# Context attention of a two-layer decoder: dividing by the softmax sums behind the weighted values, and a feed-forward issued two steps ahead

## Chip, cores and metric
The kernel runs on one core of one Trainium2 chip. The metric is the device time of one execution in microseconds (us). It is written for the engines directly: TensorE (PE in the profile), VectorE (DVE), ScalarE (ACT), GpSimd (POOL) and SyncE (SP, which issues all DMAs). Each engine executes its own instructions in the order in which the program lists them, and semaphores hold an instruction back until another engine's has finished.

## What is computed
The input `x` is 4 batches of 512 rows of 128 numbers. Six blocks follow one another, each with a layer norm in front and a residual add behind. The change touches the last two.

```python
# fifth block: 16 heads of width 8 over a context of 32 rows per batch
q = query @ Wq + bq;  k, v = split(context @ Wkv + bkv)
scores = einsum('bhid,bhjd->bhij', q, k) * 8 ** -0.5
attn = softmax(where(mask, -inf, scores));  out = einsum('bhij,bhjd->bhid', attn, v)
x = x + merge_heads(out) @ Wout + bout
# sixth block: every linear layer quantizes its input and weight in blocks of 16
scale = maximum(max(abs(xb)) / 6, 1e-12);  xq = nearest_fp4(xb / scale) * scale
h = silu(fp4_linear(ln(x), w_gate)) * fp4_linear(ln(x), w_up)      # 352 wide
x = x + fp4_linear(h, w_down)
```

## The kernel before
The kernel goes through its blocks as stages; the last three overlap at their edges: stage D (the windowed attention of the fourth block), stage E (the context attention) and stage F (the feed-forward). `x` stays in SBUF as `X[:, b]`. PSUM has eight banks of 512 float32 columns, and a planner (`psum_jobs`, `place_jobs`) goes through a list of jobs in the order in which TensorE issues them, gives each the next bank of a named pool, and turns what the bank's last user must have finished into TensorE's waits. There are no costs or due times in it: the order is the order of the lists.

**Stage E** has 16 steps, one for each tile of 128 rows: step n is batch n // 4, tile n % 4. One step is this chain: TensorE multiplies the queries with `KX`, in which each head's keys are laid out so that 16 heads x 32 context rows come out side by side, 512 columns (`eS`, L1755). VectorE scales, adds the mask (L1845) and takes the maximum of each head (L1849). GpSimd subtracts it (L1916). ScalarE takes the exponential (L1819). VectorE sums each head (L1855) and takes the reciprocal (L1856). GpSimd multiplies the tile by it (`normalized`, L1910). TensorE transposes the tile in four pieces (`eT`, L1787), and ScalarE copies them to `PTE` (L1805). When the four tiles of a batch are there, TensorE multiplies them with the values (`eO`, L1763: four accumulated matmuls, each with weights of 128 columns that are zero but for four heads), ScalarE copies the result (`out_copy`, L1810), TensorE projects (`eX`, L1770), VectorE adds to `X` and takes the statistics of the next norm (L2595, L2515, L2518), ScalarE makes the inverse deviation (`rstd`, L2384, L2386), VectorE normalizes (L2525) and quantizes (`quantize_y`, nine instructions from L1949 to L1964), TensorE transposes (`fX`, L1747) and ScalarE copies (L1833).

The loops of the engines are written out by hand, and all work on the same SE tiles, seven in rotation. On VectorE step n is `shift(n)`, `sums(n - 2)`, then what is left of stage D (`d_tail(n)`), then parts of a batch that is two back. TensorE transposes tile n at its step n + 2. `d_tail(7)` waits for the transposed output of stage D's last batch (`out1`, L1458), which TensorE issues after `values(0)`. The values of batch b are taken on TensorE at step 4b + 6.

**Stage F** has 8 steps, each of two tiles. In a step TensorE makes gate and up (`fG`, `fU`, L1975), ScalarE takes SiLU of the gate (L2011), VectorE multiplies the two into the SBUF tile `HF` (L2037) and does the first part of the quantization (L1949 to L1958: reduce, scale, reciprocal, divide, exponent, step, add), GpSimd does the last two instructions of it (L1928, L1934), TensorE transposes `HQ` (`fT`, L2003), ScalarE copies (L2018, L2019), TensorE multiplies with the down weights (`fD`, L1984) and VectorE adds to `X` (L2049, for step n - 2, right behind L2037). TensorE's order in step n is gate and up of n + 1, down of n - 1, transposes of n. Before step 0 three batches have been quantized, and the fourth is quantized in step 2. All jobs of stage F share the eight banks in rotation. SP writes a batch out when its four tiles are final.

The constants, among them the 512-column mask `vhead` with which GpSimd lays out the values `VX` (one instruction per batch), come in one DMA at the start, on which ScalarE's first instruction waits.

## Time and profile before

| | us |
|---|---|
| median of 3 runs | 1257.46 (1251.67 to 1261.60) |
| profiled execution, its own time | 1253.11 |
| span of the profiled execution | 1251.3 |
| mean granted clock of TensorE | 0.955 of full |
| busy in the span: PE / DVE / ACT / POOL | 1121.6 / 903.5 / 878.4 / 627.0 |

The busy shares are means over stages that have different limits; the stages that the change touches are the last 165 us, where the first instruction of stage E on VectorE starts at 1088.46 us and that of stage F at 1174.97 us. In a row of the timeline stand start, duration, engine, line, operation, what it writes and reads, and in brackets how long the engine had been idle and what released it. A matrix product of float32 shows twice as many instructions as the source issues.

### The profile page before, as it was taken

Reading aid. Unit: us, or ns where it says so; the run is one execution under the profiler, and the core shown is the slowest. Engines: PE = TensorE matmul, PEld = TensorE weight load, DVE = VectorE, ACT = ScalarE, POOL = GpSimd, SP = SyncE. Lnnn points to the kernel's source line nnn. Section 1 sums busy time; section 2 is a strip of 40 time slices with the busy share of each in tenths; the row PEclk is TensorE's granted clock in tenths of the full one; section 3 lists DMA queues with packets and bytes.
Section 4 is the critical chain, followed back from the end, with each engine's and each line's share of the span. In section 5 each row is a group of like instructions: output and inputs, shape, how many; then the busy total and the mean of one; then the engine's idle time right before and its main releaser. Section 6 shows DMA issues by size and latency. Waiting matters only on the chain.

```text
span 1251.3 us, 17047 instructions
## 1 busy us (share of the span) xinstructions
PE 1121.6 (90%) x6055; PEld 581.0 (46%) x6055; DVE 903.5 (72%) x1756; ACT 878.4 (70%) x1150; POOL 627.0 (50%) x463
## 2 busy tenths in 40 slices
PE   6999999999999999987888888799988999985765
PEld 3344444444444444432233332277765667653444
DVE  6776677666776677756898988456646777878885
ACT  2999999999979997882666777654655667742411
POOL 2877777777767776693454654014330300154232
PEclk9999999999999998996899999999998999997977
DMA  7200000000000000020000000000001000000000
GB/s 179 70 1 1 1 1 1 1 1 1 1 0 1 1 1 1 1 69 1 18 1 1 1 1 1 1 1 1 1 5 60 1 1 1 1 1 0 1 9 25
DMA packets 25695, 14.48 MB, mean 12 GB/s; under 512 B 14622, under 2 KB 24460, under 8 KB 25484
## 3 DMA queue, kind: packets, MB, share of 16 engines
q1 hardware_dynamic: 25612, 13.39, 3.8%
q8 instruction: 49, 0.80, 0.3%
q14 instruction: 34, 0.28, 0.1%
HBM read 12.34 MB, written 1.05 MB: 11 GB/s over the span
## 4 chain that ended last, share of the span: by engine, by line
PE 33%; POOL 29%; issue 18%; DVE 16%; ACT 2%; POOLq 0%; DMA 0%; SPq 0%; ACTq 0%; DVEq 0%
DVE ARENA L1170 6%; POOL ARENA L2730 6%; POOL ARENA L2728 5%; POOL ARENA L2724 5%; PE PS L1041 5%; POOL ARENA L2754 3%; POOL WQ L2741 3%; PE PS L911 3%; PE PS L1425 2%; PE PS L1015 2%; PE PS L1449 2%; PE PS L843 2%; PE PS L1416 2%; PE PS L859 2%; POOL WQ L2737 2%
## 5 line engine op out<-in xcount | busy, mean ns | idle before, releaser
L2580 DVE TENSOR_SCALAR ARENA<-PS,ARENA 128x512 f32<-128x512 f32 x256 | 171.9, 742 | 51.9 <-PE PS L2217 51.5
L1170 DVE TENSOR_REDUCE ARENA<-PS 128x1 f32<-128x512 f32 x256 | 160.7, 682 | 27.6 <-PE PS L859 26.9
L1086 ACT ACTIVATE ARENA<-PS 128x1024 f32<-128x1024 f32 x128 | 128.7, 1025 | 60.3 <-PE PS L897 60.0
L2398 ACT ACTIVATE ARENA<-ARENA 128x2048 f32<-128x2048 f32 x64 | 121.9, 1911 | 51.6 <-DVE ARENA L2580 51.0
L2217 PE MATMUL PS<-ARENA 64*128 64x512 f32 x512 | 139.7, 644 | 0.0
L2405 ACT ACTIVATE ARENA<-ARENA,consts_sb 128x2048 f32<-128x2048 f32 x64 | 124.7, 1995 | 0.4
L2227 PE MATMUL PS<-ARENA 128*64 128x512 f32 x512 | 119.3, 609 | 1.5 <-issue 1.5
L2411 ACT ACTIVATE ARENA<-ARENA 128x2048 f32<-128x2048 f32 x64 | 118.4, 1899 | 0.0
L1351 POOL TENSOR_TENSOR ARENA<-ARENA 128x512 f32<-128x512 f32 x32 | 40.7, 1270 | 119.8 <-DVE ARENA L1309 119.3
L2737 POOL TENSOR_SCALAR WQ<-ARENA,consts_sb 128x512 bf16<-128x512 f32 x32 | 22.2, 692 | 146.5 <-DVE ARENA L2556 146.5
L859 PE MATMUL PS<-ARENA 32*128 32x512 bf16 x256 | 71.9, 404 | 26.1 <-DVE ARENA L1170 20.7
L2556 DVE TENSOR_SCALAR ARENA<-PS 128x512 f32<-128x512 f32 x32 | 22.1, 691 | 97.5 <-PE PS L2192 97.5
L911 PE MATMUL PS<-ARENA 128*32 128x512 f32 x512 | 71.7, 632 | 9.3 <-issue 8.4
L2730 POOL TENSOR_TENSOR ARENA<-ARENA 128x1024 f32<-128x1024 f32 x32 | 76.0, 2374 | 2.5
L2728 POOL TENSOR_TENSOR ARENA<-ARENA 128x1024 f32<-128x1024 f32 x32 | 75.8, 2368 | 0.0
L2724 POOL TENSOR_TENSOR ARENA<-ARENA 128x1024 f32<-128x1024 f32 x32 | 75.6, 2362 | 0.0
L2227 PEld LDWEIGHTS PS<-ARENA 128*64 128x64 f32 x512 | 34.8, 139 | 81.8 <-issue 81.8
L1323 POOL TENSOR_SCALAR ARENA<-ARENA,consts_sb 128x512 bf16<-128x512 f32 x32 | 21.7, 692 | 96.4 <-ACT ARENA L1068 96.4
L1041 PEld LDWEIGHTS PS<-W,ARENA 128*128 128x128 f32 x512 | 59.5, 192 | 21.2 <-issue 18.9
L1117 ACT ACTIVATE ARENA<-PS,ARENA 128x512 f32<-128x512 f32 x64 | 40.4, 684 | 37.5 <-PE PS L1015 37.4
L1041 PE MATMUL PS<-W,ARENA 128*128 128x128 f32 x512 | 65.3, 281 | 0.8 <-ACT ARENA L1117 0.7
L859 PEld LDWEIGHTS PS<-ARENA 32*128 32x128 bf16 x256 | 17.6, 92 | 103.7 <-DVE ARENA L1170 63.6
(301 smaller groups left out, 2589.7 us busy)
## 6 DMA issues: line engine op xcount, KB each, us to landing
ARENA<-in_window_bias_dram SPq DMA_DIRECT2D x1, 1536.0 KB, 6.4
WKVG<-in_L_attn_W_in_dram SPq DMA_DIRECT2D x3, 384.0 KB, 5.4
X<-in_x_dram SPq DMA_DIRECT2D x4, 256.0 KB, 3.9
W<-in_L_ffn_w_dram SPq DMA_DIRECT2D x1, 1024.0 KB
out_dram<-X SPq DMA_DIRECT2D x4, 256.0 KB, 2.3
BV<-in_L_attn_b_in_dram SPq DMA_DIRECT2D x1, 512.0 KB, 6.1
Wout<-in_L_attn_W_out_dram SPq DMA_DIRECT2D x1, 512.0 KB, 4.8
WQ<-in_L_attn_wq_dram SPq DMA_DIRECT2D x1, 512.0 KB, 3.5
```

What stands on the lines that cost most here:

```text
L1041: mm = pe.matmul(o[:, t * P:(t + 1) * P], H1[:, i % 2, c, t * P:(t + 1) * P], W2[:, e, c, :], start=c == 0, stop=c == 1)
L1086: act.activation(PT[m % PT_SLOTS], bank(("cP", m)), ACT.Exp, scale=0.5).then_inc(sem("c_exp"), 1)
L1170: dve.tensor_reduce(NMX[:, w % 2, t, h:h + 1], bank(("cS", n, j)), AX.X, ALU.max, negate=True).then_inc(sem("c_max"), 1)
L2217: done(pe.matmul(banks[c], SK[r, u % 2, kt * P:(kt + 1) * P], MQ[r, u % 2, :], start=False, stop=True), ("S", u, c))
L2227: mm = pe.matmul(o[hd * 64:hd * 64 + 64, :], VA[:, u % 3, kt, hd * 64:hd * 64 + 64], D[:, u % 2, kt, hd, :], start=kt == 0, stop=kt == QT - 1)
L2398: act.activation(chunk(u, half), chunk(u, half), ACT.Sqrt).then_inc(sem("rooted"), 1)
L2405: act.activation(chunk(u, half), chunk(u, half), ACT.Ln, bias=const("eps_w")).then_inc(sem("logged"), 1)
L2411: act.activation(chunk(u, half), chunk(u, half), ACT.Exp, scale=-2.0).then_inc(sem("w_ready"), 1)
L2580: dve.tensor_scalar(D[:, u % 2, kt, hd, :], bank(("S", u, c)), K2[:, u % 2, kt, hd:hd + 1], 1e-30, ALU.add, ALU.max).then_inc(sem("guarded ...
L2724: pool.tensor_tensor(WSUM[:, u % 2], D[:, u % 2, 0], D[:, u % 2, 1], ALU.add).then_inc(sem("w_paired"), 1)
L2728: pool.tensor_tensor(WPAIR, D[:, u % 2, 2], D[:, u % 2, 3], ALU.add).then_inc(sem("w_paired"), 1)
L2730: pool.tensor_tensor(WSUM[:, u % 2], WSUM[:, u % 2], WPAIR, ALU.add).then_inc(sem("w_summed"), 1)
```

## The change
In stage E the exponentials are no longer divided by their sums before the transposes. TensorE transposes them as they are, one step earlier (tile n at step n + 1, waiting for `e_exp`), and the SE tiles are six. The values are now laid out as 32-column blocks, one for each group of four heads, so that `eO` is four matmuls of 32 output rows each, and a second product of the same form with the new, 32-column `vhead` gives the sums of the heads, repeated over each head's eight rows (`eZ`). ScalarE inverts them (`invert_sums`: Ln, then Exp of minus that), and VectorE multiplies `eO` by it (`weighted`), in place of ScalarE's copy. `sums` on VectorE and `normalized` on GpSimd are gone. The stages of a batch are issued later: the projection one batch later than the values, the add two steps further, `normalize` and `quantize_y` behind that, so that only batches 0 and 1 are quantized before stage F and batches 2 and 3 within its steps 1 and 2.

In stage F gate and up are issued two steps ahead, and TensorE's order in step n is down of n - 1, gate and up of n + 2, transposes of n. Each kind of job has banks of its own (`fT` two, `fG` two, `fU` four), and the product with the down weights goes to the free columns of the `fT` banks. The product of SiLU and up is written back to the banks of `fU`, with the block maxima beside it, and read from there. The add for step n - 2 sits behind the division. In the last step VectorE does what GpSimd did, in two halves, and transposes, copies, products and adds follow by halves.

The diff, cut to its core:

```diff
-    for g in range(4):
-        vmask[:, g, :] = (part[None, :] // DX == (4 * g + head)[:, None])
-    cols["vhead"] = vmask.reshape(P, -1)
+    cols["vhead"] = (part[:, None] // CK == np.arange(4 * DX)[None, :] // DX).astype(np.float32)
...
+    def values(b, pool):
+        return [(("eO", b), 1, [("e_o", b + 1)], pool), (("eZ", b), 1, [("e_sum", b + 1)], pool)]
+
+    def project_out(b, pool):
+        return [(("eX", b), 1, [("x_new", 4 * B + b + 1)], pool)]
+
     jobs = scores(0, "E3") + scores(1, "E3")
...
+    for s in range(steps + 1):
         jobs += d_tail(s)
         for n in scores_at(s):
             jobs += scores(n, pool_at(s))
...
+        if s >= 1:
+            b, t = divmod(s - 1, QT)
+            jobs += [(("eT", s - 1), 1, [("e_pt", s)], pool_at(s))]
             if t == 1 and b:
...
+                jobs += values(b - 1, pool_at(s))
+            if t == 1 and b >= 2:
+                jobs += project_out(b - 2, pool_at(s))
+            if s == FIRST_QUANTIZED:
+                jobs += [(("fX", 0), 1, [("f_x", 1)], pool_at(s))]
+    jobs += values(B - 1, "E2") + gate_and_up_jobs(0) + project_out(B - 2, "E01") + project_out(B - 1, "E01")
+    return jobs + [(("fX", 1), 1, [("f_x", 2)], "fG")]
+
+
+FIRST_QUANTIZED = 15
 
 
 def gate_and_up_jobs(n):
...
+    return [(("fG", n), 2, [("f_silu", n + 1)], "fG"), (("fU", n), 2, [("f_scaled", n + 1)], "fU")]
...
+    jobs = gate_and_up_jobs(1)
+    last = B * QT // 2 - 1
+    for n in range(last + 1):
+        if n in QUANTIZED_AT:
+            jobs += [(("fX", QUANTIZED_AT[n]), 1, [("f_x", QUANTIZED_AT[n] + 1)], "fG")]
+        if n + 2 <= last:
+            jobs += gate_and_up_jobs(n + 2)
+        if n < last:
+            jobs += [(("fT", n), 2, [("f_ht", n + 1), ("x_final", n + 1)], "fT")]
+        else:
+            jobs += [(("fL", j), 1, [("f_ht", last + 1 + j)], "fG") for j in range(2)]
+    return jobs
+
+
+QUANTIZED_AT = {2: B - 2, 4: B - 1}
...
             def values(b):
                 pe.wait_ge(sem("e_pt"), QT * (b + 1))
-                pe.wait_ge(sem("e_vx"), b + 1)
+                pe.wait_ge(sem("e_vx"), 1)
                 o = begin(("eO", b))
                 for g in range(4):
-                    mm = pe.matmul(o, VX[b][:, g, :], PTE[:, b % 2, g, :], start=g == 0, stop=g == 3)
+                    r = slice(32 * g, 32 * g + 32)
+                    mm = pe.matmul(o[r, :], VX[:, b, r], PTE[:, b % 2, g, :], start=True, stop=True)
                 done(mm, ("eO", b))
+                o = begin(("eZ", b))
+                for g in range(4):
+                    r = slice(32 * g, 32 * g + 32)
+                    mm = pe.matmul(o[r, :], const("vhead"), PTE[:, b % 2, g, :], start=True, stop=True)
+                done(mm, ("eZ", b))
...
+            for s in range(STEPS + 1):
                 d_tail(s)
                 for n in scores_at(s):
                     scores(n)
...
+                if s < 1:
                     continue
...
+                n = s - 1
                 b, t = divmod(n, QT)
...
+                pe.wait_ge(sem("e_exp"), n + 1)
                 o = begin(("eT", n))
...
+                p = SE[n % 6].rearrange("p h j -> p (h j)")
                 for g in range(4):
                     mm = pe.transpose(o[:, g * P:(g + 1) * P], p[:, g * P:(g + 1) * P], ident)
                 done(mm, ("eT", n))
...
+                if t == 1 and b:
                     values(b - 1)
...
+                if t == 1 and b >= 2:
+                    project_out(b - 2)
+                if s == FIRST_QUANTIZED:
+                    turn_quantized(pe, begin, done, 0)
+            values(B - 1)
             pe.wait_ge(sem("f_w"), 3)
             gate_and_up(pe, begin, done, 0)
...
+            project_out(B - 2)
             project_out(B - 1)
...
+            turn_quantized(pe, begin, done, 1)
...
+            def invert_sums(b):
+                full(act, ("eZ", b))
+                if b:
+                    act.wait_ge(sem("e_o"), b)
+                act.activation(ISUM, bank(("eZ", b)), ACT.Ln).then_inc(sem("e_sum"), 1)
+                act.wait_ge(sem("e_sum"), b + 1)
+                act.activation(ISUM, ISUM, ACT.Exp, scale=-1.0).then_inc(sem("e_isum"), 1)
+
+            for n in range(STEPS + 2):
                 b, t = divmod(n, QT)
                 d_tail(n)
...
                 if n < STEPS:
                     act.wait_ge(sem("e_shift"), n + 1)
...
+                    act.activation(SE[n % 6], SE[n % 6], ACT.Exp).then_inc(sem("e_exp"), 1)
+                if n >= 2:
+                    turned(n - 2)
+                if t == 3 and b:
+                    invert_sums(b - 1)
+                if t == 2 and b >= 2:
+                    rstd(5, b - 2)
+                if n == FIRST_QUANTIZED + 1:
+                    quantized_out(act, 0)
+            invert_sums(B - 1)
+            silu(act, 0)
...
-            def sums(n):
-                dve.wait_ge(sem("e_exp"), n + 1)
-                if n >= 3:
-                    dve.wait_ge(sem("e_p"), n - 2)
-                link(dve.tensor_reduce(SUE[:, n % 3], SE[n % 7], AX.X, ALU.add))
-                dve.reciprocal(RCE[:, n % 3], SUE[:, n % 3]).then_inc(sem("e_rc"), 1)
...
+            def weighted(b):
+                full(dve, ("eO", b))
+                dve.wait_ge(sem("e_isum"), b + 1)
+                if b >= 2:
+                    full(dve, ("eX", b - 2))
+                dve.tensor_tensor(OTE[:, b % 2], ISUM, bank(("eO", b)), ALU.mult).then_inc(sem("e_o"), 1)
+
+            def add(b):
+                dve.wait_ge(sem("xb4"), b + 1)
+                add_to_stream(4, b, ("eX", b))
+                stats(5, b)
+
+            for n in range(STEPS):
                 b, t = divmod(n, QT)
...
+                shift(n)
                 d_tail(n)
...
+                if t == 1 and b >= 2:
+                    weighted(b - 2)
+                if t == 3 and b >= 2:
+                    add(b - 2)
+                if t == 0 and b == 3:
+                    normalize(5, 0)
+                if t == 1 and b == 3:
+                    quantize_y(dve, link, 0)
+            normalize(5, 1)
+            weighted(B - 2)
+            quantize_y(dve, link, 1)
+            weighted(B - 1)
             hidden(dve, link, 0, None)
...
+            add(B - 2)
+            add(B - 1)
...
+            pool.tensor_tensor(VX.rearrange("p b (g c) -> p (b g) c", g=4),
+                               V4.rearrange("p b (g c) -> p (b g) c", g=4),
+                               const("vhead").unsqueeze(1).to_broadcast([P, 4 * B, 4 * DX]), ALU.mult).then_inc(sem("e_vx"), 1)
...
-            def normalized(n):
-                pool.wait_ge(sem("e_rc"), n + 1)
-                pool.tensor_tensor(SE[n % 7], SE[n % 7], RCE[:, n % 3].unsqueeze(2).to_broadcast([P, HX, CK]),
-                                   ALU.mult).then_inc(sem("e_p"), 1)
...
-            for n in range(STEPSF):
+            for n in range(STEPSF - 1):
...
+            def down(n, halves=(0, 1)):
+                for j in halves:
+                    pe.wait_ge(sem("f_ht"), n + 1 + (j if n == last else 0))
                     for c, (r0, k) in enumerate(FCH):
...
+                        mm = pe.matmul(sum_of(n, j), HQT[0:k, n % 2, j, c * P:(c + 1) * P], WD[0:k, c, :],
                                        start=c == 0, stop=c == 2)
...
+                    if n == last or j == 1:
+                        mm.then_inc(sem("f_d"), 1)
+
+            def turn_half(o, n, j):
+                for c, (r0, k) in enumerate(FCH):
+                    mm = pe.transpose(o[0:k, c * P:(c + 1) * P], HQ[:, n % 2, j, r0:r0 + k], ident)
+                return mm
+
+            gate_and_up(pe, begin, done, 1)
             for n in range(STEPSF):
...
+                if n in QUANTIZED_AT:
+                    turn_quantized(pe, begin, done, QUANTIZED_AT[n])
                 if n:
                     down(n - 1)
...
+                if n + 2 < STEPSF:
+                    gate_and_up(pe, begin, done, n + 2)
+                if n < last:
+                    pe.wait_ge(sem("f_hq"), n + 1)
+                    o = begin(("fT", n))
+                    for j in range(2):
+                        mm = turn_half(o[:, j, :], n, j)
+                    done(mm, ("fT", n))
+                else:
+                    for j in range(2):
+                        pe.wait_ge(sem("f_hq"), n + 1 + j)
+                        done(turn_half(begin(("fL", j)), n, j), ("fL", j))
+            for j in range(2):
+                down(last, (j,))
...
+            quantized_out(act, 1)
+            silu(act, 1)
+            act.preload_act_table_set("natural_log_exp_and_others")
+            rstd(5, B - 2)
+            rstd(5, B - 1)
+            turned(0)
+            silu(act, 2)
+            for n in range(1, last):
+                if n in QUANTIZED_AT:
+                    quantized_out(act, QUANTIZED_AT[n])
+                if n + 2 < STEPSF:
+                    silu(act, n + 2)
                 turned(n)
+            act.wait_ge(sem("f_d"), last - 1)
+            for j in range(2):
+                full(act, ("fL", j))
+                act.copy(HQT[:, last % 2, j, 0:2 * P], bank(("fL", j))[:, 0:2 * P])
+                act.copy(HQT[0:96, last % 2, j, 2 * P:3 * P], bank(("fL", j))[0:96, 2 * P:3 * P]).then_inc(sem("f_ht"), 1)
...
+            rows = bank(("fU", n))
+            h = rows[:, :, 0:FI]
+            dve.tensor_tensor(h, SG[:, n % 2], h, ALU.mult).then_inc(sem("f_h"), 1)
+            dve.wait_ge(sem("f_h"), n + 1)
+            scratch = X_SCRATCH[n % 2]
+            blocks = FI // BLK
+            v = h.rearrange("p t (k i) -> p t k i", i=BLK)
+            amax = rows[:, :, FI:FI + blocks]
+            sc, rc = (scratch[0][:, k, 0:2 * blocks].rearrange("p (t k) -> p t k", t=2) for k in (1, 2))
+            A, M, T = scratch[1:4]
+            link(dve.tensor_reduce(amax, v, AX.X, ALU.max, apply_absolute_value=True))
             if n >= 2:
...
+                dve.wait_ge(sem("f_hq"), n - 1)
+            link(dve.tensor_scalar(sc, amax, float(np.float32(1 / 6)), 1e-12, ALU.mult, ALU.max))
+            link(dve.reciprocal(rc, sc))
+            dve.scalar_tensor_tensor(out=A.rearrange("p (t k i) -> p t k i", t=2, i=BLK), in0=v, scalar=1.0 - 2.0 ** -24,
+                                     in1=rc.unsqueeze(3).to_broadcast([P, 2, blocks, BLK]),
+                                     op0=ALU.mult, op1=ALU.mult).then_inc(sem("f_scaled"), 1)
+            if n >= 1:
+                add()
+            dve.wait_ge(sem("f_scaled"), n + 1)
+            link(dve.tensor_scalar(M.bitcast(U32), A.bitcast(U32), 0x7F800000, None, ALU.bitwise_and))
+            link(dve.tensor_scalar(M, M, 1.0, 3.0 * 2.0 ** 21, ALU.max, ALU.mult))
+            dve.tensor_tensor(T, A, M, ALU.add).then_inc(sem("f_added"), 1)
...
+            def between(n):
+                if n >= 2:
+                    add(n - 2)
+                if n in (1, 2):
+                    normalize(5, B - 3 + n)
+                    quantize_y(dve, link, B - 3 + n, n)
+
+            for n in range(1, STEPSF):
+                hidden(dve, link, n, lambda: between(n))
+            scratch = X_SCRATCH[last % 2]
+            by = lambda t, j: t[:, j * FI:(j + 1) * FI].rearrange("p (k i) -> p k i", i=BLK)
+            blocks = FI // BLK
+            dve.wait_ge(sem("f_added"), last + 1)
+            link(dve.tensor_tensor(scratch[3], scratch[3], scratch[2], ALU.subtract))
+            full(dve, ("fT", last - 2))
+            hq = HQ[:, last % 2].rearrange("p t n -> p (t n)")
+            for j in range(2):
+                scales = scratch[0][:, 1, j * blocks:(j + 1) * blocks].unsqueeze(2).to_broadcast([P, blocks, BLK])
+                if j:
+                    dve.wait_ge(sem("f_hq"), last + 1)
+                else:
+                    dve.wait_ge(sem("f_hq"), last)
+                dve.tensor_tensor(by(hq, j), by(scratch[3], j), scales, ALU.mult).then_inc(sem("f_hq"), 1)
+            add(last - 1)
+            b, t = divmod(2 * last, QT)
+            for j in range(2):
+                dve.wait_ge(sem("f_d"), last + 1 + j)
+                dve.tensor_tensor(X[:, b, t + j], X[:, b, t + j], sum_of(last, j), ALU.add).then_inc(sem("x_final"), 1)
```

## Rows read from the trace of the kernel before
**Rows 1.** Windows: stretch, length, busy us (instructions) PE, PEld, DVE, ACT, POOL, clock, DMA.
```profile
1083.80:1127.00 43.20, 36.23 (x154) 20.68 (x152) 34.12 (x76) 21.10 (x62) 18.90 (x18) 0.99 0.00 1
1127.00:1169.00 42.00, 25.18 (x86) 14.03 (x86) 34.76 (x80) 13.41 (x27) 17.05 (x17) 0.77 0.00 0
1169.00:1239.80 70.80, 50.88 (x218) 36.02 (x218) 62.92 (x105) 18.00 (x31) 22.02 (x16) 0.83 0.04 12
1239.80:1251.30 11.50, 4.47 (x18) 3.74 (x18) 0.42 (x1) 0.85 (x2) 2.76 (x2) 0.59 0.07 23
```
**Rows 2.** Timeline of VectorE in stage E: the sums of a tile, and two waits.
```profile
1102.95 0.68 DVE L1855 TENSOR_REDUCE ARENA<-ARENA 128x16 f32<-128x512 f32 x1
...
1103.84 0.63 DVE L1845 SCALAR_TENSOR_TENSOR ARENA<-PS,BXV 128x512 f32<-128x512 f32 x1
...
1119.30 0.69 DVE L2595 TENSOR_TENSOR X<-X,PS 128x512 f32<-128x512 f32 x1 [6.39 <-PE PS L1458]
...
1143.95 0.69 DVE L1845 SCALAR_TENSOR_TENSOR ARENA<-PS,BXV 128x512 f32<-128x512 f32 x1 [3.64 <-PE PS L1755]
```
**Rows 3.** Groups by line, shapes apart, from 960 us to the end.
```profile
L1910 POOL TENSOR_TENSOR ARENA<-ARENA 128x512 f32<-128x512 f32 x16 | 17.8, 1113 | 3.9 <-DVE ARENA L1856 3.9
...
L1958 DVE TENSOR_TENSOR ARENA<-ARENA 128x704 f32<-128x704 f32 x8 | 7.1, 893 | 0.3
...
L2037 DVE TENSOR_TENSOR ARENA<-ARENA,PS 128x704 f32<-128x704 f32 x8 | 7.1, 882 | 4.7 <-PE PS L1975 4.4
```
**Rows 4.** Costliest groups of the page, whole span: other stages' instructions of similar form.
```profile
L2580 DVE TENSOR_SCALAR ARENA<-PS,ARENA 128x512 f32<-128x512 f32 x256 | 171.9, 742 | 51.9 <-PE PS L2217 51.5
...
L911 PE MATMUL PS<-ARENA 128*32 128x512 f32 x512 | 71.7, 632 | 9.3 <-issue 8.4
```
**Rows 5.** Timeline of TensorE: values of batches 0 and 1.
```profile
1115.13 3.70 PE L1763 MATMUL PS<-ARENA,WQ 128*128 128x512 f32 x8 [0.39 <-ACT ARENA L1805]
...
1134.82 5.89 PE L1763 MATMUL PS<-ARENA,WQ 128*128 128x512 f32 x8
```
**Rows 6.** Timeline of VectorE in stage F.
```profile
1187.63 3.66 DVE L2525 TENSOR_SCALAR Y<-X,MV,RSTD 128x128 f32<-128x128 f32 x4
...
1203.65 0.88 DVE L2037 TENSOR_TENSOR ARENA<-ARENA,PS 128x704 f32<-128x704 f32 x1
...
1209.45 0.89 DVE L2037 TENSOR_TENSOR ARENA<-ARENA,PS 128x704 f32<-128x704 f32 x1
...
1211.50 1.08 DVE L1952 TENSOR_SCALAR ARENA<-ARENA 128x44 f32<-128x44 f32 x1
...
1218.97 0.89 DVE L2037 TENSOR_TENSOR ARENA<-ARENA,PS 128x704 f32<-128x704 f32 x1 [2.96 <-PE PS L1975]
```
**Rows 7.** Timeline of GpSimd in stage F.
```profile
1209.40 1.68 POOL L1928 TENSOR_TENSOR ARENA<-ARENA 128x704 f32<-128x704 f32 x1 [9.31 <-DVE ARENA L1958]
1211.15 1.38 POOL L1934 TENSOR_TENSOR ARENA<-ARENA 128x704 f32<-128x704 f32 x1
```
**Rows 8.** Timeline of TensorE in stage F.
```profile
1212.59 1.54 PE L2003 MATMUL PS<-consts_sb,ARENA 128*128 128x128 f32 x6 [3.71 <-POOL ARENA L1934]
...
1220.05 0.82 PE L2003 MATMUL PS<-consts_sb,ARENA 128*128 128x128 f32 x6
1220.70 2.53 PE L1975 MATMUL PS<-WKVG,ARENA 128*128 128x352 f32 x8
1223.07 1.50 PE L1984 MATMUL PS<-Wout,ARENA 128*128 128x128 f32 x12
...
1245.17 2.93 PE L1984 MATMUL PS<-Wout,ARENA 128*128 128x128 f32 x12 [0.94 <-ACT ARENA L2019]
```
**Rows 9.** Timeline of VectorE: the last two instructions.
```profile
1239.35 0.41 DVE L2049 TENSOR_TENSOR X<-X,PS 128x256 f32<-128x256 f32 x1
1248.14 0.42 DVE L2049 TENSOR_TENSOR X<-X,PS 128x256 f32<-128x256 f32 x1 [8.38 <-PE PS L1984]
```
**Rows 10.** Chain that ended last, start of the program: start, us, what.
```profile
1.24 4.44 DMA consts_sb<-in_consts_dram
```

183 lines of the change are left out of this document (30 added, 153 removed).

## Prediction
> **What bounds the kernel now.** I read the windows first, for the stages that the change touches. From 1127 us on TensorE is busy 25.18 of 42.00 us and then 50.88 of 70.80, at a granted clock of 0.77 and 0.83, and GpSimd and ScalarE less than half of the time. VectorE is busy 34.76 and 62.92 [rows 1]: it sets the pace, and about 4 of the 15.1 us that it lacks are gaps between linked instructions. Then VectorE's timeline, for its waits: 6.39 us for stage D's last output, 3.64 for scores [rows 2], 2.96 for gate and up [rows 6]. Between its two adds at the very end there are 8.38 us with nothing to do, the chain of the last step through GpSimd, TensorE and ScalarE [rows 9]. So there are four terms: the start, what delays 1119.30, the 120.05 us from there to 1239.35, and the 11.95 us from there to the end of the span.
>
> **Start.** The constants are 448 columns narrower of some 930. Their DMA takes 4.44 us and ends on the chain that ended last [rows 10]. Half the bytes can't save half of it, since the statistics of the first batch come in beside them: 0.5 us, between 0 and 1.
>
> **Before 1119.30.** VectorE waits for the transposes of stage D's output, and TensorE has `values(0)` in front of them: 3.70 us [rows 5]. The new form is eight source matmuls, 16 recorded ones, of 32 output columns. The nearest row is stage C's, 512 of this very form in 71.7 us busy, 0.14 each although one lasts 632 ns, so four column groups run side by side [rows 4]. That is 8 x 0.14 = 1.1 us for `eO`, 1.1 for `eZ`, and 1.5 less. The transposes no longer wait for a sum (0.89 from one instruction to the next [rows 2]) and a multiplication on GpSimd (1.1 [rows 3]), but tile 5 is transposed in front as well (half a us). I take -2.0; 0 if stage D's own work decides, -4 if all adds up.
>
> **From there to the last hidden step (120.05 us).** Removed from VectorE: ten sums (tiles 6 to 15; the others lie in front) x 0.89 = 8.9. Added: four `weighted`, each a 512-column product with a PSUM source like L2595, 0.69 [rows 2]: 2.8. Net -6.1. GpSimd's multiplications, ScalarE's copies and `VX` are off the path and cost or save nothing there: POOL is busy 17.05 of 42 us [rows 1]. ScalarE gets two activations per batch (0.6 to 0.7 each) for one copy; three of the four are covered by its own slack, the fourth is counted below.
>
> Port conflicts: the 44-column instruction at 1211.50 took 1.08 us and ended 0.05 behind GpSimd's L1934 at 1212.53, so it was held until GpSimd had finished [rows 6, 7]. Four short normalizing instructions took 3.66 us in the same way [rows 6]. Counted over stages E and F this makes some 10.9 us: 1 to 1.3 for each of three norms behind L1910, two times 0.5 in `quantize_y`, and 6.5 in stage F. After the change L1910 is gone, the scales of a hidden step are computed from PSUM, and the division reads PSUM; I keep 2.5, for norms behind the shift that stays on GpSimd. -8.4, with ends of 0 (the PSUM forms are held too, and other norms fall beside GpSimd) and -10.9.
>
> Waits of VectorE now: 11.2. New ones, with t = 0 at the new 1119.30. VectorE does add, two shifts, `normalize(4,3)` (held 1 us), `weighted(0)`, shifts 10 and 11 and stands at `add(0)` at 9.8. TensorE can begin the transposes of that norm at 6.5, then tile 9, `values(1)` and only then `project_out(0)`: at the half clock, in which `values(1)` now runs (5.89 against 3.70 [rows 5]), 1.1 + 1.1 + 3.6 + 1.4, so 14. **4.2 us of wait.** The inverse deviation of that batch sits in ScalarE's order ahead of its copy of the last queries, so the scores for shift 12 come another 2.5 later. Then `normalize(5,1)` and `weighted(2)`, one behind the other behind the loop, wait for ScalarE 0.6 and 1.6; the last sums and the table load in front of `silu(0)` leave some 2; 1 more for TensorE in stage F. In all 12: +0.8. Ends: 6 (full clock, short queue) and 20 (each wait lasts as long as 3.64 did, or 2.96, in six places).
>
> The quantizations of batches 2 and 3 only move; each is nine instructions in either place. But they now sit in the middle of hidden steps 1 and 2, behind which `f_added` is late for GpSimd, and gate and up are by then two steps ahead: nothing waits.
>
> Writing the product to PSUM is shown by no row. The reading product with PSUM source takes 882 ns against 893 from SBUF [rows 3], so 0 for reads. Upper bound: the scalar operation of rows 4, 742 ns for 512 columns, scaled to 704: 1.02 us, 0.14 over 0.88, three accesses in eight steps: 3.4. I take 0, the row of the same form. The Trainium skill says otherwise ("VectorE: DVE Perf Modes", on the errata): a VectorE instruction has a fixed cost of 58 cycles from SBUF and 120 from PSUM, which speaks against keeping the product there. By that rule three accesses would cost an estimated 0.2 us a step, 1.6 us in all. The 882 and 893 ns of rows 3 don't bear it out.
>
> In steps 3 to 7 of stage F, VectorE's own length is 5.80 (1203.65 to 1209.45 [rows 6]). TensorE's is a new loop, because `down` now stands directly behind ScalarE's copy of the transposes: 0.82 + about 1.15 for the copies + 1.50 + 2.53 [rows 8] = 6.0. The lead of two steps covers the difference five times over, 1 us. This term: -6.1 - 8.4 + 0.8 = -13.7.
>
> **End.** Now 11.95 us from 1239.35 [rows 9], of which 2.75 lie behind the last add. In between are GpSimd's 3.1 [rows 7], transposes 1.5, copies 0.95, products 2.93 at half clock [rows 8] and semaphores. New: subtraction 0.89, one half 0.5, the second 0.5, transposes 0.45, copies 0.6, products 0.75 to 1.5, add 0.3, semaphores 0.5, so about 4.8. 11.95 - 2.75 - 4.8 = 4.4, taken as -4.3 (ends -2.5 and -5.5).
>
> **Sum**: -0.5 - 2.0 - 13.7 - 4.3 = -20.5. Against the profiled execution's 1253.11 this is 1232.6, against the median of 1257.46 it is 1237. The runs spread over 10 us, so I take 1236.
>
> **Rivals.**
> - *The waits come back.* Same mechanism, but the serial places take 20 us instead of 12 and the port conflicts return half: +8 + 3, 1247, about 1% under the median. For it: ScalarE's order has `rstd` and the copies between exponentials, TensorE's clock is already 0.77 there. Against: most of VectorE's 16 shifts need nothing of them. Chance 0.18.
> - *Larger gain*: waits of 6 instead of 12, 4 us in front: 1228. For it: TensorE has 5 us less work in `values`. Chance 0.13.
> - *Slower: TensorE's loop in stage F.* Place: `down`, gate and up, transposes in one serial round with ScalarE's copy inside. If the clock stays at the half level, a round is 1.54 + 1.15 + 2.93 + 5.06 = 10.7 instead of 6.0 [rows 8]; over seven rounds +33, so 1269. It decides from a round of about 9.0, where the 20.5 are used up ((9.0 - 6.0) x 7 = 21). Against it: the round leaves TensorE idle for 1.1 us at a time, while the half-clock rows stand behind idle times of 3.71 us [rows 8]. Chance 0.05.
> - *The products don't run side by side.* If the 16 records cost 0.46 each as in rows 5, `values` takes 7.4 instead of 2.2, on the path at three places: +15.6, 1252. Rows 4 speak against it. Chance 0.04.
>
> **Numbers.** The forecast has 0.60. Its own range is 1230 to 1242; with the rivals at both sides and the spread of the runs the range is 1223 to 1250. A change of less than 1% (12.6 us, so down to 1244.9) can't be told from none. Faster by over 1%: forecast, larger gain and a third of the first rival, 0.80. Within: 0.15. Slower by over 1%: 0.05.
>
> **What would show it.** The 6.39 us wait in front of stage D's last add shrinks to 2 to 4 us plus what VectorE arrives earlier. `eO` and `eZ` show 16 records in 2 to 4 us. A wait of 3 to 5 us on L1770's successor in front of `add(0)`. Hidden steps 3 to 7 start 5.8 to 6.2 us apart with no 1.08 us instruction, and the clock of TensorE in stage F is over 0.9. From the last addition of step 7 to the end 7 to 9 us instead of 11.95. I am wrong if VectorE still waits for over 18 us in all, or if a step of stage F takes over 7.

## Result and the profile after the change

The kernel after takes 1237.82 us (median of 4 runs, 1234.46 to 1239.04), the kernel before 1258.31 us beside it (4 runs): ratio 0.9845 [0.9804, 0.9886]. A second comparison gave 1234.67 against 1255.44 us, ratio 0.9851 [0.9811, 0.9890]. The forecast was 1236 us within 1223 to 1250, and 20.5 us of gain; the differences of the medians are 20.5 and 20.8 us. The execution profiled after took 1239.04 us with a span of 1237.2.

The two spans differ by only 14.1 us. The stages that the change does not touch explain the rest. VectorE's first shift of scores, where stage E begins for it, stands at 1088.46 us before and at 1092.87 after, 4.4 us later; from there to the end it is 162.84 us before and 144.33 after, 18.5 us less. In the twelve further profiles the same first shift lies anywhere from 1084.56 to 1097.94 us, while the length behind it repeats to a few tenths where neither code nor clock differs: 144.33, 143.96 and 144.04 us in three profiles of the same work. Of the kernel before there is one profile only, so how far its own 162.84 us would repeat isn't known. Every number below therefore counts from that shift or from stage D's last add to the stream, and not from the start of the span.

The windows of the kernel after, cut at the same times as [rows 1] as far as the shorter span allows (stretch, length, busy us and instructions of PE, PEld, DVE, ACT, POOL, clock, DMA share, GB/s):

```profile
1083.80:1127.00 43.20, 38.01 (x186) 22.25 (x184) 29.14 (x58) 24.12 (x68) 10.89 (x11) 1.00 0.00 1
1127.00:1169.00 42.00, 29.17 (x142) 15.10 (x142) 30.45 (x67) 17.75 (x34) 8.39 (x8) 0.80 0.00 1
1169.00:1230.00 61.00, 38.10 (x186) 28.52 (x187) 57.65 (x113) 16.01 (x30) 21.41 (x14) 0.85 0.05 14
1230.00:1237.20 7.20, 4.15 (x24) 3.52 (x22) 1.73 (x5) 1.06 (x4) 0.00 (x0) 0.74 0.12 36
```

GpSimd's busy time in stage E is halved (17.05 to 8.39 us in the second line). In stage F VectorE is busy 57.65 of 61.00 us, 95%, where it was 62.92 of 70.80: it is still what sets the pace, with less idle time. TensorE's clock is hardly higher than before, 0.80 and 0.85.

TensorE in front of stage D's last add, timeline. The values of batch 0 are the first line and the sums the second:

```profile
1119.52 1.06 PE L1769 MATMUL PS<-ARENA,WQ 128*32 128x512 f32 x8
1120.40 1.04 PE L1774 MATMUL PS<-ARENA,consts_sb 128*32 128x512 f32 x8
1121.37 0.66 PE L1464 MATMUL PS<-consts_sb,ARENA 128*128 128x128 f32 x4
```

The 16 records take 1.9 us together, where eight took 3.70 [rows 5]: eight records that write 32 partitions each, of about 0.6 us, fit into 1.06 us, so the column groups run side by side. They still stand in front of the transposes (third line) that the add needs.

VectorE from that add to the first hidden step, timeline; a number in brackets is the wait before the instruction, with what ended it:

```profile
1122.06 0.69 DVE L2663 TENSOR_TENSOR X<-X,PS 128x512 f32<-128x512 f32 x1 [4.92 <-PE PS L1464]
...
1126.60 1.84 DVE L2593 TENSOR_SCALAR Y<-X,MV,RSTD 128x128 f32<-128x128 f32 x4
...
1135.36 0.69 DVE L2663 TENSOR_TENSOR X<-X,PS 128x512 f32<-128x512 f32 x1 [3.69 <-PE PS L1781]
...
1139.73 0.69 DVE L1859 SCALAR_TENSOR_TENSOR ARENA<-PS,BXV 128x512 f32<-128x512 f32 x1 [2.36 <-PE PS L1760]
...
1153.21 0.69 DVE L2663 TENSOR_TENSOR X<-X,PS 128x512 f32<-128x512 f32 x1 [0.74 <-PE PS L1781]
...
1155.82 1.12 DVE L2593 TENSOR_SCALAR Y<-X,MV,RSTD 128x128 f32<-128x128 f32 x4 [0.60 <-ACT RSTD L2454]
1158.03 0.69 DVE L1870 TENSOR_TENSOR ARENA<-ARENA,PS 128x512 f32<-128x512 f32 x1 [1.09 <-issue]
...
1164.49 0.69 DVE L1870 TENSOR_TENSOR ARENA<-ARENA,PS 128x512 f32<-128x512 f32 x1 [0.75 <-ACT ARENA L1826]
...
1166.51 0.90 DVE L2069 TENSOR_TENSOR PS<-ARENA,PS 128x704 f32<-128x704 f32 x1 [1.32 <-ACT ARENA L2030]
```

The wait for stage D's output is 4.92 us instead of 6.39 [rows 2]. Behind it stand the waits that the forecast placed: 3.69 in front of the first new add, 2.36 in front of shift 12, and small ones behind the loop.

Stage F, timelines of VectorE and, in the second block, of GpSimd:

```profile
1205.25 0.90 DVE L2069 TENSOR_TENSOR PS<-ARENA,PS 128x704 f32<-128x704 f32 x1
1206.18 0.90 DVE L2077 TENSOR_REDUCE PS<-PS 128x44 f32<-128x704 f32 x1
1207.12 0.20 DVE L2080 TENSOR_SCALAR ARENA<-PS 128x44 f32<-128x44 f32 x1
1207.35 0.43 DVE L2081 RECIPROCAL ARENA<-ARENA 128x44 f32<-128x44 f32 x1
...
1211.33 0.90 DVE L2069 TENSOR_TENSOR PS<-ARENA,PS 128x704 f32<-128x704 f32 x1 [0.22 <-PE PS L1982]
```
```profile
1205.20 1.68 POOL L1939 TENSOR_TENSOR ARENA<-ARENA 128x704 f32<-128x704 f32 x1 [2.71 <-DVE ARENA L2090]
1206.95 1.39 POOL L1945 TENSOR_TENSOR ARENA<-ARENA 128x704 f32<-128x704 f32 x1
```

The 44-column instruction runs inside GpSimd's second product and takes 0.20 us; in the kernel before it took 1.08 in the one step of [rows 6] and 1.07 in another. The reciprocal behind it reads SBUF, also inside that product, and isn't lengthened: 0.43 us, as without GpSimd beside it. The five hidden steps that begin with step 3 start 5.84, 6.08, 5.85 and 5.84 us apart.

The end, VectorE's and TensorE's timelines:

```profile
1229.68 1.08 DVE L2123 TENSOR_TENSOR ARENA<-ARENA 128x352 f32<-128x352 f32 x2
...
1233.56 0.29 DVE L2128 TENSOR_TENSOR X<-X,PS 128x128 f32<-128x128 f32 x1 [1.99 <-PE PS L1995]
```
```profile
1230.90 1.49 PE L2002 MATMUL PS<-consts_sb,ARENA 128*128 128x128 f32 x6
```

The wait of 8.38 us between the last two adds [rows 9] has become a subtraction and the multiplication in two halves on VectorE itself (first line: the halves) and a wait of 1.99. The last transposes take 1.49 us, about what they took at the half clock in [rows 8]; the clock here is 0.69 in the 5.5 us behind hidden step 7.

One table carries the comparison. "Front" is from the first shift to stage D's last add, "middle" from there to the end of hidden step 7, "busy" VectorE's busy time in the middle, "waits" the sum of its bracketed waits there, "end" the rest of the span. The rows below the second are the experiments of the next section.

| kernel | front | middle | busy | waits | end | all |
|---|---|---|---|---|---|---|
| before | 30.84 | 120.13 | 104.80 | 11.20 | 11.87 | 162.84 |
| after | 29.19 | 106.66 | 91.68 | 10.77 | 8.48 | 144.33 |
| after, again | 29.19 | 106.29 | 91.61 | 10.48 | 8.48 | 143.96 |
| wider constants | 29.20 | 106.29 | 91.59 | 10.50 | 8.55 | 144.04 |
| eight sums back | 29.20 | 109.85 | 96.78 | 8.60 | 8.52 | 147.57 |
| multiplication on GpSimd back | 29.19 | 109.20 | 94.47 | 10.58 | 9.56 | 147.95 |
| product in SBUF | 29.19 | 111.97 | 97.80 | 9.89 | 9.60 | 150.76 |
| lead of one step | 29.18 | 131.01 | 91.59 | 35.68 | 10.57 | 170.76 |
| last step through GpSimd | 29.19 | 108.23 | 91.70 | 12.33 | 11.85 | 149.27 |
| down last | 29.20 | 105.01 | 91.61 | 9.14 | 8.76 | 142.97 |
| rstd a step later | 29.19 | 102.89 | 91.63 | 7.07 | 8.51 | 140.59 |
| the same, second profile | 29.20 | 102.52 | 91.54 | 6.85 | 7.45 | 139.17 |
| values and rstd a step later | 27.19 | 106.82 | 90.69 | 11.98 | 7.41 | 141.42 |
| the same, rstd ahead | 27.19 | 103.64 | 91.60 | 7.85 | 7.48 | 138.31 |

The end varies with TensorE's clock alone where its code is the same: 7.4 to 7.5 us in three profiles at 1.00 behind step 7, 8.5 at 0.69, 9.6 at 0.55 and 0.60, and 10.6 at 0.50 (lead of one step). So that part of a difference in the last two columns is clock and not the edit.

### The profile page after: what moved, and what is told of

The parts are those of the page before. It is cut to its first block, busy times and chain, and to the rows that moved or that the text cites. A ratio compares the mean times of both kernels' runs of the same rounds, so it can differ in the third digit from the quotient of the medians.

```text
span 1237.2 us, 17060 instructions
## 1 busy us (share of the span) xinstructions
PE 1116.8 (90%) x6087; PEld 575.5 (47%) x6087; DVE 888.1 (72%) x1732; ACT 881.2 (71%) x1156; POOL 604.0 (49%) x442
## 4 chain that ended last, share of the span: by engine, by line
PE 35%; POOL 27%; DVE 18%; issue 16%; ACT 3%; DMA 0%; POOLq 0%; DVEq 0%; ACTq 0%
DVE ARENA L1176 6%; POOL ARENA L2798 6%; POOL ARENA L2796 5%; POOL ARENA L2792 5%; PE PS L1047 5%; POOL ARENA L2822 3%; POOL WQ L2809 3%; PE PS L917 3%; PE PS L1431 2%; PE PS L849 2%; PE PS L1021 2%; PE PS L1455 2%; PE PS L1422 2%; PE PS L865 2%; POOL WQ L2805 2%
```

## Experiments

Each kernel is the kernel after with one edit, unless the text says otherwise.

**The narrower constants.** 480 unused columns bring the width back.

```
     cols["xhead"] = ...
+    cols["unused"] = np.zeros((P, 480))
```

> The changed kernel with 480 unused columns of constants added, so that the first DMA is as large as it was before. If the smaller DMA at the start is worth 0.5 us, ScalarE's first instruction starts 0.5 us later than in the changed kernel (5.2 us), and the first scores of the first block as well. The rival says that the start is set by the first batch's own DMA and statistics: no difference. In neither case does anything behind the first block move by more than executions differ.

Median 1231.1 us (2 runs), ratio 0.9791 [0.9752, 0.9830]: no loss. The constants landed in 4.4 us before, 3.1 after and 3.7 here, although before and here they are the same 465 KB, and ScalarE's first activation, at 5.71 before, shows why that is free (its timeline, the kernel after and this one):

```profile
5.20 0.30 ACT L2452 ACTIVATE RSTD<-MV,consts_sb 128x4 f32<-128x4 f32 x1 [3.19 <-DVE MV L2586]
```
```profile
5.10 0.30 ACT L2453 ACTIVATE RSTD<-MV,consts_sb 128x4 f32<-128x4 f32 x1 [3.09 <-DVE MV L2587]
```

In both it waits for the statistics (MV) and not for the constants. The half microsecond between the kernels is there in the traces, but the width doesn't bring it back; why the transfer took 4.4 us in the one profile before stays open.

**The sums.** Reduction and reciprocal on VectorE, with results that nobody reads, for tiles 6 to 13 behind stage D's add (and tiles 0 to 5 in front).

```
+                if n >= 2:
+                    sums(n - 2)
                 d_tail(n)
```

> The changed kernel with the two removed VectorE instructions per tile put back (sum of each head and its reciprocal, tiles 0 to 13, results unused). If VectorE's own work is what the stage is made of, the eight tiles behind stage D's last add cost 8 x 0.89 = 7.1 us less what falls into its waits: the sums of steps 10 and 11 disappear in the 3.69 us wait in front of the first context add, so about +5 us between that add of stage D (1122.06) and the end of hidden step 7 (1228.72), 106.7 us now. If the waits for TensorE and ScalarE set the pace, under +2 us.

Median 1242.02 us, ratio 0.9881 [0.9850, 0.9911]. The middle is 3.2 us longer, between the 5 of the theory and the under 2 of its rival. VectorE's timeline:

```profile
1123.45 0.68 DVE L1881 TENSOR_REDUCE ARENA<-ARENA 128x16 f32<-128x512 f32 x1
1124.16 0.25 DVE L1882 RECIPROCAL ARENA<-ARENA 128x16 f32<-128x16 f32 x1
1124.33 0.63 DVE L1861 SCALAR_TENSOR_TENSOR ARENA<-PS,BXV 128x512 f32<-128x512 f32 x1
...
1126.48 1.18 DVE L2602 TENSOR_SCALAR Y<-X,MV,RSTD 128x128 f32<-128x128 f32 x4
...
1134.56 0.69 DVE L2672 TENSOR_TENSOR X<-X,PS 128x512 f32<-128x512 f32 x1 [1.96 <-PE PS L1783]
```

One sum takes 0.88 us of VectorE (1123.45 to 1124.33), eight take 7.0. Two things give about half of it back: the waits fall by 2.2 us, above all that of 3.69 to 1.96, and the two norms that fell beside GpSimd's subtraction no longer do (1.18 against 1.84 for the one shown, 1.3 us for both). So the removed work was worth less than its duration, mostly because a wait follows it.

**The multiplication on GpSimd.** It writes to an unused tile, behind each exponential; VectorE waits for it before it overwrites that exponential's tile six steps later.

```
+                if n >= 2:
+                    pool.wait_ge(sem("e_exp"), n - 1)
+                    pool.wait_ge(sem("e_p"), n - 2)
+                    pool.tensor_tensor(DUM, SE[(n - 2) % 6], ..., ALU.mult).then_inc(sem("e_p"), 1)
```

> The changed kernel with GpSimd's multiplication of each tile put back at its old place (behind the subtraction of the tile two later), writing to an unused tile. VectorE only has to wait for it before it overwrites a tile six steps later. If port conflicts of VectorE with GpSimd were a part of the gain, the normalizing and scaling instructions beside it get longer by up to 1 us each: +2 to +4 us between stage D's last add and the end of hidden step 7. If GpSimd is simply off the path: 0. If its queue matters (its subtraction comes 1 us later): scores tiles reach ScalarE later and the 3.69 us wait grows by 1.

Median 1238.70 us, ratio 0.9858 [0.9828, 0.9888]. Middle +2.5, VectorE's busy time +2.8 with the same 191 instructions, waits about the same. (The end is 1.1 longer, which is the clock.) VectorE's timeline has the place:

```profile
1126.88 3.25 DVE L2600 TENSOR_SCALAR Y<-X,MV,RSTD 128x128 f32<-128x128 f32 x4
```

The four normalizing instructions take 3.25 us instead of 1.84: GpSimd now works without a gap from 1126.73 to 1129.79, in three instructions, and three of the four end within 0.1 us of the end of one of them. The add behind comes 1.3 us later. So the price is VectorE held; GpSimd's queue being late would have lengthened the first wait, which is 3.56 us against 3.69.

**The product in SBUF.** Product, maxima and division use SBUF again.

```
-            dve.tensor_tensor(h, SG[:, n % 2], h, ALU.mult)
+            dve.tensor_tensor(HF, SG[:, n % 2], h, ALU.mult)
```

> The changed kernel with the product of SiLU and up written to an SBUF tile, as before, and the block maxima too; the semaphores are as in the changed kernel. If reading from PSUM keeps VectorE free of GpSimd, the 44-column scaling instruction, which starts 1.9 us into a step, waits again until GpSimd's second instruction ends 3.2 us into it: about +1.3 us in each of the steps 2 to 7 that have GpSimd's work beside them, a step of 7.1 us instead of 5.83, +6 to +8 us in all. If the PSUM form is only as fast as the SBUF form and nothing else, 0. If a PSUM access costs more, as the fixed costs in the Trainium skill (VectorE: DVE Perf Modes) would have it, this version is faster by 0.2 us a step.

Median 1244.94 us, ratio 0.9903 [0.9870, 0.9935]: of all edits that keep the order of the work this costs most. VectorE's timeline of stage F, and GpSimd's in the last block:

```profile
1204.70 0.89 DVE L2070 TENSOR_TENSOR ARENA<-ARENA,PS 128x704 f32<-128x704 f32 x1
1205.62 0.89 DVE L2078 TENSOR_REDUCE ARENA<-ARENA 128x44 f32<-128x704 f32 x1
1206.55 1.28 DVE L2081 TENSOR_SCALAR ARENA<-ARENA 128x44 f32<-128x44 f32 x1
...
1208.32 0.89 DVE L2083 SCALAR_TENSOR_TENSOR ARENA<-ARENA 128x704 f32<-128x704 f32 x1
```
```profile
1206.40 1.38 POOL L1946 TENSOR_TENSOR ARENA<-ARENA 128x704 f32<-128x704 f32 x1
```

Only the 44-column instruction changes: 1.28 us instead of 0.20, and it ends 0.05 us behind GpSimd's product. Steps 3 to 7 start 6.90 or 6.91 us apart instead of 5.84. In the middle VectorE is busy 6.1 us longer, six times 1.07 us less a little, and waits 0.9 less: that is its +5.3. The theory had taken 1.3 us a step and 6 to 8 in all; it had the place right and the size too large. The three wide accesses cost 0.89 here and 0.90, 0.90 and 0.89 in PSUM, so the third theory, that PSUM costs 0.2 us a step, finds 0.02.

**The lead of two steps.** Gate and up products one step ahead, as before, and ScalarE's SiLU with them.

```
-                if n + 2 < STEPSF:
-                    gate_and_up(pe, begin, done, n + 2)
+                if n + 1 < STEPSF:
+                    gate_and_up(pe, begin, done, n + 1)
```

> The changed kernel with gate and up issued one step ahead instead of two (TensorE: down of n - 1, gate and up of n + 1, transposes of n). If the lead of two steps is what keeps VectorE from waiting in stage F, gate and up of step n + 1 now come only behind GpSimd's end of step n - 1, the transposes, ScalarE's copies (1.15 us) and the down products (1.5): 3.7 + 0.8 + 1.15 + 1.5 + 1.3 for the gate + 0.8 for SiLU is 9.2 us into a step of 5.83, so VectorE waits some 3.4 us in each of steps 3 to 7, +15 to +20 us. If the banks of their own for each kind of job are what matters, under +3 us.

Median 1265.58 us, ratio 1.0066 [1.0041, 1.0090]: slower than the kernel before. VectorE's busy time is unchanged (91.59 us), its waits rise from 10.8 to 35.7, more than the 15 to 20 us expected. Its timeline, and TensorE's behind it:

```profile
1230.32 0.90 DVE L2068 TENSOR_TENSOR PS<-ARENA,PS 128x704 f32<-128x704 f32 x1 [6.74 <-PE PS L1982]
```
```profile
1221.80 1.52 PE L2002 MATMUL PS<-consts_sb,ARENA 128*128 128x128 f32 x6 [4.02 <-DVE X L2098]
```

In the kernel after and here the down product lies in the banks of the transposes, so the transposes of a step wait for VectorE's add of the step before (4.02 us; the expectation had left this out), and gate and up of the next step stand behind them. A round is then 10.9 to 12.7 us. In the kernel after the same wait is there (1.36 us in front of the transposes of step 6), but there gate and up of the next step have gone ahead. I read from this that the second step of lead pays for the shared banks; no run has one step of lead with separate banks, so how much of the 24.9 us the sharing makes isn't shown.

**The last step.** Through GpSimd and in one piece again.

```
-            for n in range(STEPSF - 1):
+            for n in range(STEPSF):
...
+            add(last - 1)
+            add(last)
```

> The changed kernel with its last step done as all others: GpSimd does the last two quantizing instructions, and transposes, copies, down products and add come in one piece. If the forecast's reckoning of the end holds, GpSimd's 3.1 us takes the place of VectorE's 1.4 to the first half, and the pipelining by halves is gone: about +3.5 us from the end of hidden step 7 to the end of the span (8.5 us now), so 12. The rival, that the halves bring nothing because each small instruction has its fixed cost, says +1.7.

Median 1238.32 us (2 runs), ratio 0.9859 [0.9819, 0.9899]; the medians don't resolve it, the profile does. The end is 11.85 us instead of 8.48, +3.4 at nearly the same clock (0.71 and 0.69), with the old wait back (VectorE's timeline):

```profile
1236.97 0.42 DVE L2085 TENSOR_TENSOR X<-X,PS 128x256 f32<-128x256 f32 x1 [6.64 <-PE PS L1992]
```

The middle, which this edit doesn't touch, is 1.6 us longer because one step takes 7.73 us; on that step see the experiment on TensorE's loop.

**Inverse deviation a step later.** In the kernel after ScalarE's `rstd(5, 0)` waits 4.79 us for the statistics with the copy of the last queries behind it (ScalarE's timeline of the kernel after):

```profile
1137.41 0.30 ACT L2452 ACTIVATE RSTD<-MV,consts_sb 128x4 f32<-128x4 f32 x1 [4.79 <-DVE MV L2586]
...
1137.85 0.67 ACT L1537 ACTIVATE ARENA<-PS,BN 128x512 f32<-128x512 f32 x1
```

```
-                if t == 2 and b >= 2:
+                if t == 3 and b >= 2:
                     rstd(5, b - 2)
```

> The changed kernel with ScalarE's inverse deviation of a batch (two short activations that wait for the context add) one step later in its order, behind the copy of the last queries. If the waits of VectorE at the first context add and at shift 12 come from this serial order, the copy of the queries is no longer held from 1136.1 to 1137.9, shift 12 starts 1.1 us earlier (wait 2.36 becomes 1.2), and the values of the last batch 1 us earlier: -1 to -2.5 us. If TensorE is the cause, 0.

> The kernel after with ScalarE's rstd(5, b) one step later, repeated in the same call as the kernel with the later values, to compare the two improved versions on one chip. Expected: 140.6 us from the first scores shift to the end again (every variant has repeated to tenths of a microsecond there), median ratio to before 0.976 to 0.983; if the version with later values and rstd ahead of invert_sums works, this one is 3 to 5 us slower than it.

Median 1230.29 us (2 runs), ratio 0.9795 [0.9763, 0.9827], and in a second comparison 1231.67 us (6 runs), ratio 0.9833 [0.9806, 0.9859]. All behind stage D's add is 3.7 and 5.2 us shorter than in the kernel after, where 1 to 2.5 was expected. VectorE's timeline of the first:

```profile
1131.29 0.69 DVE L1859 SCALAR_TENSOR_TENSOR ARENA<-PS,BXV 128x512 f32<-128x512 f32 x1 [0.69 <-PE PS L1760]
...
1148.15 1.11 DVE L2593 TENSOR_SCALAR Y<-X,MV,RSTD 128x128 f32<-128x128 f32 x4 [1.97 <-ACT RSTD L2454]
```

The wait for shift 12 falls from 2.36 to 0.69. The gain beyond the expectation lies behind it: five waits of 4.50 us in all in the kernel after have become one of 1.97, for the second `rstd`, moved too, in front of the norm of batch 1, and one of 0.38.

The two profiles of this one kernel also differ, by 1.6 us between stage D's add and the first new one (13.29 and 11.67 us). TensorE's timeline of the values, first the first profile, then the second:

```profile
1124.21 1.94 PE L1769 MATMUL PS<-ARENA,WQ 128*32 128x512 f32 x8
1125.92 1.48 PE L1774 MATMUL PS<-ARENA,consts_sb 128*32 128x512 f32 x8
```
```profile
1125.88 1.06 PE L1769 MATMUL PS<-ARENA,WQ 128*32 128x512 f32 x8
1126.76 1.04 PE L1774 MATMUL PS<-ARENA,consts_sb 128*32 128x512 f32 x8
```

The second holds the upper level of 2.4 GHz, in the first the clock has fallen toward 1.2 GHz in this stretch, in front of which TensorE had waited 2.90 us in both. The windows from 5 to 10 us behind stage D's add, in the same order:

```profile
1120.30:1125.30 5.00, 2.89 (x20) 1.90 (x24) 4.53 (x8) 2.81 (x7) 2.14 (x3) 0.81 0.01 2
```
```profile
1122.33:1127.33 5.00, 2.88 (x28) 1.71 (x28) 4.54 (x8) 2.81 (x7) 2.14 (x3) 1.00 0.01 2
```

VectorE, ScalarE and GpSimd do the same work; TensorE's busy time is the same too, but at the granted clock of 0.81 it gets through 20 records where at 1.00 it gets through 28. The second profile's end is 1.1 us shorter for the same reason, and one of its steps in stage F is 0.8 longer (7.04 against 6.20): 3.7 us is what the edit itself shows.

**Values a step later as well**, so that stage D's transposes go first. The projection now stands in front of the values, and the first `invert_sums` runs at ScalarE's step 8.

```
-                if t == 1 and b:
-                    values(b - 1)
...
+                if t == 2 and b:
+                    values(b - 1)
```

> The changed kernel with ScalarE's inverse deviation one step later, and on TensorE the projection of the batch before in front of the values, and the values one step later than now (with their inversion at ScalarE's step 8 for batch 0). If the serial places found in the changed kernel cost what they show, stage D's transposed output comes 2.1 us earlier (eO and eZ no longer in front of it), the 3.69 us wait for the first context add nearly goes, and shift 12 comes about 4 us earlier: -4 to -7 us against the changed kernel. The rival: VectorE's waits only move to the next place (the values and their inverted sums come later, so weighted() waits), and it is within 2 us.

Median 1232.88 us, ratio 0.9829 [0.9802, 0.9856]. Stage D's add comes 2.0 us earlier and its wait is 2.91 instead of 4.92, but the whole is 141.42 us: 2.9 less than the kernel after, not the 4 to 7 expected, and more than with `rstd` alone. VectorE's timeline, then ScalarE's:

```profile
1133.99 1.12 DVE L2594 TENSOR_SCALAR Y<-X,MV,RSTD 128x128 f32<-128x128 f32 x4 [3.49 <-ACT RSTD L2455]
...
1151.68 1.11 DVE L2594 TENSOR_SCALAR Y<-X,MV,RSTD 128x128 f32<-128x128 f32 x4 [5.09 <-ACT RSTD L2455]
```
```profile
1132.27 0.60 ACT L1824 ACTIVATE ARENA<-PS 128x512 f32<-128x512 f32 x1 [3.40 <-PE PS L1774]
```

The inverse deviation (at 1133.43) stands behind `invert_sums` (the row shown), which waits for the later sums. So the next kernel turns the two round on ScalarE:

```
                 if t == 3 and b >= 2:
+                    rstd(5, b - 2)
                     invert_sums(b - 1)
-                    rstd(5, b - 2)
```

> Change of the kernel after: the values and sums products of batches 0 to 2 are issued one step later, invert_sums(0) runs at step 8, and ScalarE takes rstd(5, b) at step t = 3, now AHEAD of invert_sums(b + 1) instead of behind it. Theory (what held the previous attempt back was the order of these two on ScalarE: the values products that invert_sums waits for are a step later, and the normalizing of VectorE queued behind them for 3.49 and 5.09 us): both waits fall to about 1 us, so from the first scores shift to the end 135 to 137.5 us instead of 141.4 there and 140.6 with rstd(5, b) moved alone; stage D's last add stays at about +27.2. Rival (the waits are set by the statistics themselves or by TensorE's products, not by the queue of ScalarE): 140 to 142 us, as before.

Median 1232.09 us (4 runs), ratio 0.9821 [0.9803, 0.9838]; 138.31 us from the first shift on, inside neither theory (135 to 137.5; 140 to 142). The cause of the two waits was the queue: the wait of 3.49 us is gone and that of 5.09 is down to 0.82, but 2.73 us have moved on to the product of the weighted values (VectorE's timeline):

```profile
1148.94 1.11 DVE L2594 TENSOR_SCALAR Y<-X,MV,RSTD 128x128 f32<-128x128 f32 x4 [0.82 <-ACT RSTD L2455]
...
1152.78 0.69 DVE L1871 TENSOR_TENSOR ARENA<-ARENA,PS 128x512 f32<-128x512 f32 x1 [2.73 <-issue]
```

Its stretch is 6.0 us shorter than that of the kernel after, 1.0 of it by the clock in the end. It is 2.3 us shorter than the first profile with `rstd` alone and 0.9 shorter than the second, which has the same full clock at the values and in the end; 3 to 5 were expected. All four medians of these variants (1230.29 to 1232.88) lie below both of the kernel after (1234.67 and 1237.82), but so does that of the padded kernel (1231.1), which does the same work as the kernel after, and the intervals of the ratios overlap. That they are faster is shown in the stretch, not in the time of the whole.

**The order of TensorE's loop.** Gate and up of step n + 2 stand before the down product of step n - 1.

```
-                if n:
-                    down(n - 1)
                 if n + 2 < STEPSF:
                     gate_and_up(pe, begin, done, n + 2)
+                if n:
+                    down(n - 1)
```

> The kernel after with TensorE's loop of the feed-forward reordered: the gate and up products of step n + 2 stand before the down product of step n - 1, not behind it. My theory (VectorE sets the hidden steps at 5.84 us each, TensorE has room in every step): hidden steps 3 to 7 stay at 5.8 to 5.9 us, and the time within 1 us of after. Rival (TensorE's loop is as near to being the bound as VectorE's, at a half clock in part of the stage): some steps grow or shrink by 0.5 us or more, 2 us or more in all.

Median 1237.62 us, ratio 0.9868 [0.9839, 0.9897]. From the first new add to the end of step 7 it is 93.34 us, in the kernel after 93.36. Its steps 3 to 7 start 5.84, 5.84, 6.87 and 5.85 us apart. These four add up to 24.4 us, against 23.6 in the kernel after and 23.8 in its repetition, so stage F is 0.6 to 0.8 us longer here. The equal sum comes from the wait of 0.74 us in front of the second add, which this profile lacks, as does the kernel after in its repetition.

One step longer than 5.85 is in every profile with a lead of two steps but that of the product in SBUF, and it has two causes. In the kernel after (6.08) and in others (6.24, 7.04, 7.73) VectorE waits there for gate and up, and TensorE is at the lower clock: 0.54 in the 7 us around the step of 7.04. Here the clock is 1.00 throughout the step of 6.87. VectorE waits for the down product, which now stands behind gate and up, and these had waited for ScalarE's copy of the quantized rows (VectorE's timeline, then TensorE's):

```profile
1210.01 0.42 DVE L2099 TENSOR_TENSOR X<-X,PS 128x256 f32<-128x256 f32 x1 [0.94 <-PE PS L1995]
```
```profile
1206.03 2.60 PE L1982 MATMUL PS<-WKVG,ARENA 128*128 128x352 f32 x8 [1.04 <-ACT ARENA L1847]
```

So VectorE sets the steps of 5.84, and TensorE is the next limit, when its clock is low or when the product that VectorE needs first stands second. The rival was right that a step grows by over 0.5 us, and wrong that 2 us come together.

**The kernel after, again.**

> The kernel after itself, unchanged, timed again in five rounds. Theory (the change is worth what its own stages show, 18 to 20 us, and what differs besides is scatter of the unchanged stages): median 1232 to 1239 us, ratio 0.981 to 0.988; from the first scores shift to the end 144.3 us, or 1.6 us less, since two other runs in which this stretch is the same code had the last add of stage D to the first add of the new stage once at 13.30 and once at 11.67 us. Rival (the first comparison was lucky): ratio above 0.990.

Ratio 0.9851 [0.9811, 0.9890], 143.96 us from the first shift on, 13.30 us between stage D's last add and the first new one: the theory holds.

## Why the prediction was right

**Start, -0.5.** The constants are 480 columns narrower (465 and 225 KB), not 448. The traces differ by the half microsecond, but the padded kernel starts as early, so the width isn't its reason. The term isn't confirmed and too small to matter.

**Before stage D's last add, -2.0: measured -1.65.** The step was right: `eO` and `eZ` take 1.9 us for 3.70. Its other half, that TensorE must then do more in front, holds too: with the values moved behind the transposes a further 2.0 us come free, so TensorE's order in front of this add is still what decides.

**Middle, -13.7: measured -13.5**, though its three parts were each a little off and cancel; that the sum fits to 0.2 us is luck. Work and port conflicts together were -14.5; VectorE's busy time fell by 13.1. Waits were +0.8; they fell by 0.4.
- *Port conflicts*, VectorE's instructions held beside GpSimd's, were the larger part, and the mechanism is borne out: 1.07 us a step by the product in SBUF, 2.8 us by the multiplication on GpSimd. My count of 10.9 us before was too high: against the same forms undisturbed the rows of that trace have some 9.4 us behind stage D's add, because the three norms of stage E lost 0.7 to 0.8 each and not 1 to 1.3. Of the 2.5 us that I left, 1.5 were there (two norms of 1.84 instead of 1.11). That is -7.9 for -8.4. The experiments don't split this gain: in the kernel before, the 44-column instruction was held in two steps of eight (1.08 and 1.07 us), while in the new order, where GpSimd's products lie beside VectorE's in six steps, the SBUF form is held in all six.
- *Removed sums* were taken at their full 0.89 each. The duration was right (0.88), the value was not: 7.0 us put back cost 3.2. The balance came out because I had also counted the waits that the shorter work uncovers, by their places: 4.2 forecast in front of the first add (3.69), 2.5 for shift 12 (2.36), 0.6 and 1.6 behind the loop (0.60, 1.09), 2 in front of the first step (0.75 and 1.32), 1 in stage F (0.22). Only the 0.74 in front of the second add was not among them. My reason for the second, ScalarE's order, is shown by the kernel with `rstd` later.
- *Half clock in `values(1)`* went into the 4.2 us. With the upper level the same wait is 2.06 us.
- *Writing the product to PSUM at 0*: a step now takes 5.84 us against 5.80, 0.3 us over eight steps. By the rule of the Trainium skill ("VectorE: DVE Perf Modes", on the errata) an estimated 1.6 us would have been lost; the trace doesn't agree, with 0.90 against 0.89 us for the same product. What the change of memory buys is the freedom from GpSimd. The Trainium skill ("GPSIMD Engine Reference", Specifications) says that GpSimd shares SBUF interfaces with VectorE and collides with its instructions in a two-port mode or with two SBUF inputs. The trace agrees for two inputs: in the kernel before a 512-column division with both in SBUF took 1.55 us beside GpSimd and 0.69 elsewhere. The 44-column instruction, 1.28 us from SBUF and 0.20 from PSUM, has one input, and no row shows in which mode it ran.
- *TensorE's round of 6.0 us against VectorE's 5.80, covered by the lead*: right in the kernel after, where stage F waits 0.22 us. Without the lead the kernel is slower than before, so the lead carries more than the 1 us that I gave it. My slower rival named the place and the right neighbours, but priced only the clock; the wait of the transposes for VectorE's add, 4.02 us, wasn't in it.

**End, -4.3: measured -3.4.** The wait went as forecast, and putting it back costs 3.4. I had the last transposes at the upper clock (0.45 us); they took 1.49. In the three profiles in which the clock is 1.00 there the end is 7.4 to 7.5 us, 4.4 less than before, so the term was mis-sized by the clock.

**Signs.** I expected TensorE's clock in stage F over 0.9; it is 0.85, before 0.83. That sign was wrong: VectorE sets the pace, and TensorE is busy 38.10 of 61.00 us. The wait in front of stage D's last add was to shrink to 2 to 4 us plus what VectorE arrives earlier; it is 4.92, and VectorE arrives only 0.2 earlier from the first shift, so that sign failed by 0.7, although the add itself comes nearly as much earlier as forecast. The 16 records of `eO` and `eZ` take 1.9 us, just under the 2 to 4. The other signs came in: 3.69 us in front of the first new add, steps 3 to 7 of 5.84 to 6.08, no 1.08 us instruction in steps 3 to 7, an end of 8.48 us within 7 to 9, and waits of 10.8 us in all, under 18.

The sum of the measured parts is -0.5 - 1.65 - 13.5 - 3.4 = -19.0; the medians show 20.5 and 20.8. The 1.5 us between are less than the scatter of the unchanged stages and stay unexplained. The forecast is right by its mechanism; that it meets the difference of the medians to the tenth is luck.

## What to carry over

Count a removed instruction by the wait that follows it in the same engine's order, not by its duration: here 7.0 us of work were worth 3.2, while keeping one instruction of 44 columns out of GpSimd's way was worth 1.07 us in each of six steps of the new order. When two uses share a PSUM bank, look at which engine's release the second use then waits for, and check that the work behind it has enough lead. And compare profiles from a mark in front of the changed stage, since the untouched stages moved the span by up to 13 us.

## What the runs showed of the hardware

Some VectorE instructions that read SBUF are held beside a GpSimd product until it ends, and others aren't. The 44-column scaling (TENSOR_SCALAR) took 1.28 us and ended 0.05 behind GpSimd's product, and took 0.20 with a source in PSUM; normalizing instructions (TENSOR_SCALAR, 128 columns) took up to 1.08 us each instead of 0.34. A division with two SBUF inputs took 1.55 us instead of 0.69 (kernel before, VectorE's timeline, beside GpSimd's product from 1198.70 to 1200.08):

```profile
1199.08 1.55 DVE L1954 SCALAR_TENSOR_TENSOR ARENA<-Y,ARENA 128x512 f32<-128x512 f32 x1
```

The reciprocal of 44 columns, with its one input in SBUF, took 0.43 us inside GpSimd's product as outside, and the reduction of 704 columns 0.88. The wide product, maxima and division took 0.89 or 0.90 us in either memory; the division read SBUF clear of GpSimd there. Sixteen records of TensorE that write 32 partitions each took 1.9 us at the upper clock and 3.2 to 3.4 at the lower. And one and the same kernel met either clock at the same place of its program, after the same 2.90 us of idle TensorE, which moved the next add of VectorE by 1.6 us; what decides between the two these runs don't show.
